# A feed-forward stage of its own for the last batch, in Q's weights and stage 1's PSUM banks, under a new order of all engines

## What is computed

```python
x = x + xattn(layernorm(x), ctx, ctx, Wq, Wk, Wv, Wo)      # softmax(q k^T / sqrt(32)) v, then Wo
n = layernorm(x).astype(bfloat16)
qg, sg = dynamic_quant(n, inv_gate)                        # round(n * inv / scale), scale = max|n * inv| / 127
qu, su = dynamic_quant(n, inv_up)
inter = silu(qg @ w_gate.T * sg * s_wgate) * (qu @ w_up.T * su * s_wup)
inter = clip(inter, -10, 10).astype(bfloat16)
qi, si = dynamic_quant(inter, inv_inter)
out = x + qi @ w_down.T * si * s_wdown
```

## Time and profile before

| | us |
|---|---|
| median of 3 runs | 737.89 (736.92 to 738.33) |
| profiled execution | 736.11 |
| its span | 734.3 |
| TensorE busy | 674.5 (92%) |
| VectorE busy | 480.8 (65%) |
| ScalarE busy | 285.5 (39%) |
| GpSimd busy | 260.3 (35%) |
| TensorE idle before its first matmul | 11.0 |

### The profile page before, as it was taken

How to read it: one execution, slowest core, us unless ns; L and a number is a source line. 1 busy time by engine, 2 the same in 40 slices (tenths; PEclk the granted TensorE clock), 3 DMA queues, 4 the chain that set the end, 5 groups by cost and what they waited for, 6 DMA issues and landing times.

```text
span 734.3 us, 14234 instructions
## 1 busy us (share of the span) xinstructions
PE 674.5 (92%) x5840; PEld 444.2 (60%) x5840; DVE 480.8 (65%) x772; ACT 285.5 (39%) x449; POOL 260.3 (35%) x207
## 2 busy tenths in 40 slices
PE   4999999999999999999999999999899989897743
PEld 3788988867767576656665656655566444443321
DVE  3664241762675585679676877787485877977763
ACT  5343212553534315253434444351524336243330
POOL 5533310030332224423523435241544436535431
PEclk9999999999999999999999999999999999999977
DMA  9778622787570242251325241334314252213000
GB/s 341 243 258 279 216 87 87 237 239 233 169 237 2 55 155 84 88 183 66 84 68 179 89 124 58 87 112 135 94 59 122 88 151 80 73 59 90 29 29 29
DMA packets 46239, 93.58 MB, mean 127 GB/s; under 512 B 6240, under 2 KB 22624, under 8 KB 46176
## 3 DMA queue, kind: packets, MB, share of 16 engines
q1 hardware_dynamic: 43872, 84.30, 37.5%
q0 software_dynamic: 2304, 8.39, 2.9%
HBM read 70.52 MB, written 22.02 MB: 126 GB/s over the span
## 4 chain that ended last, share of the span: by engine, by line
PE 76%; DVE 10%; DMA 4%; ACT 3%; issue 2%; POOL 2%; SPq 1%; POOLq 0%; DVEq 0%; ACTq 0%
PE bank L767 20%; PE bank L680 18%; PE bank L793 6%; PE bank L642 6%; PE bank L655 5%; PE bank_o L731 4%; PE bank L815 4%; PE bank_s L717 3%; PE bank_d L736 3%; PE bank_s L699 3%; DVE neg_max L2176 2%; DMA k_stack<-k_dram 2%; PE bank L665 2%; PE bank L781 2%; DVE amax L2211 1%
## 5 line engine op out<-in xcount | busy, mean ns | idle before, releaser
L680 PE MATMUL bank<-act_t_hi,wq_hi 128*128 128x256 f16 x512 | 139.7, 273 | 0.0
L680 PE MATMUL bank<-act_t_hi,wq_lo 128*128 128x256 f16 x512 | 139.5, 272 | 0.0
L680 PE MATMUL bank<-act_t_lo,wq_hi 128*128 128x256 f16 x512 | 139.4, 272 | 0.0
L2176 DVE TENSOR_REDUCE neg_max<-bank_s 128x4 f16<-128x512 f32 x128 | 83.6, 684 | 45.6 <-PE bank_s L699 45.0
L1607 ACT ACTIVATE probs<-bank_s 128x512 f32<-128x512 f32 x128 | 73.5, 601 | 54.3 <-PE bank_s L717 47.0
L2793 POOL TENSOR_TENSOR wv_hi<-wv_hi,wv_lo 128x512 f32<-128x512 f32 x28 | 37.4, 1343 | 106.2 <-DMA wv_lo<-r_dram 106.2
L1643 ACT COPY q_t<-bank 128x1024 f16<-128x1024 f16 (+1 forms) x48 | 41.7, 869 | 46.4 <-PE bank L781 28.5
L2787 POOL TENSOR_TENSOR xs<-xb,inv_up 128x1024 f32<-128x1024 bf16 x16 | 38.0, 2378 | 57.2 <-ACT code_g L1664 57.2
L680 PEld LDWEIGHTS bank<-act_t_hi,wq_hi 128*128 128x128 f16 x512 | 49.9, 98 | 11.0 <-issue 1.2
L680 PEld LDWEIGHTS bank<-act_t_lo,wq_hi 128*128 128x128 f16 x512 | 50.1, 98 | 9.9
L680 PEld LDWEIGHTS bank<-act_t_hi,wq_lo 128*128 128x128 f16 x512 | 50.0, 98 | 6.0
(11 more groups left out here) (145 smaller groups left out, 1391.7 us busy)
## 6 DMA issues: line engine op xcount, KB each, us to landing
q_stack<-q_dram SPq DMA_DIRECT2D x48, 256.0 KB, 4.5
inp<-in_x SPq DMA_DIRECT2D x16, 512.0 KB, 5.0
wv_lo<-r_dram SPq DMA_DIRECT2D x56, 128.0 KB, 2.8
x<-in_x SPq DMA_DIRECT2D x11, 512.0 KB, 4.4
out<-x POOLq DMA_DIRECT2D x11, 512.0 KB, 3.0
q_dram<-q_st_hi SPq DMA_DIRECT2D x8, 512.0 KB, 3.3
q_dram<-q_st_lo SPq DMA_DIRECT2D x8, 512.0 KB, 3.9
w_gate<-in_ctx_t SPq DMA_DIRECT2D x6, 512.0 KB, 5.1
```

What stands on the lines that cost most here:

```text
L680: ins = nc.tensor.matmul(bank[:, :, jj, :], wq_sb[a][:, 2 * item + jj, kc, :], act_t[m][:, kc, :, :], start=(kc == 0 and (a, m) == PARTS[0 ...
L2176: nc.vector.tensor_reduce(neg_max[:, c:c + REP], bank_s[g % 2][:, :].rearrange("p (j n) -> p j n", j=REP), AX_X, ALU.max, negate=True).the ...
```

## The change

Three things. First, batch 15 (`LAST`) takes its feed-forward tiles in the memory of Q's weights, with separate ones for the two sides where one tile served both, own columns in `amax`, `scale` and `rscale`, own semaphores, and the two banks of stage 1 instead of `bank3`, in the order projection, gate and up, down. The waits that only guard the shared tiles go for this batch, among them the one of `xs_` for `code`, of `ln2_apply` and `code` for `tq`, of `tanh` for `code_i` and of `gscale` for `fin_half`. Second, its last sum goes from GpSimd to VectorE, and each half of the columns is stored by SyncE as soon as it is added. Third, the lists of all five engines stand in another order, from the first call to the last. TensorE has the same 5840 matmuls.

```diff
 def place3(r, name):
+    if r == LAST:
+        return (W3 + G3 + T3).index(name)
     if name in W3:
...
 def before3(r, name):
+    if r == LAST:
+        i = place3(r, name) - 2
+        return (r, (W3 + G3 + T3)[i]) if i >= 0 else None
...
-        if 0 <= q < NB:
+        if 0 <= q < LAST:
...
-        amax = sb("amax", [P, 3], F32)
+        amax = sb("amax", [P, 6], F32)
...
-            return bank3[place3(r, name) % 2]
+            return (bank1 if r == LAST else bank3)[place3(r, name) % 2]
+        def spare(h, start, n, dt):
+            v = flat(wq_sb[h])[:, start:start + (n if dt in (F16, BF16) else 2 * n)]
+            return v if dt == F16 else v.bitcast(dt)
+        def xs_of(r, u):
+            return spare(("hi", "lo")[u], 0, D, F32) if r == LAST else xs[:, :]
+        def xb_of(r):
+            return spare("hi", 5 * D, D, BF16) if r == LAST else xb[:, :]
+        def codes_of(r, u):
+            if r == LAST:
+                return spare("hi", (6 if u == 0 else 5) * D, D, F16)
+            return codes[u][:, :]
+        def q_t_of(r, u):
+            if r == LAST:
+                return spare(("hi", "lo", "hi")[u], (7, 2, 7)[u] * D, D, F16).rearrange("p (c n) -> p c n", c=KC)
+            return q_t[:, :, :]
+        def gu_of(r, u):
+            return spare("hi", (2 + u) * D, FF, F32) if r == LAST else (g_buf, u_buf)[u][:, :]
+        def t_of(r):
+            return spare("hi", 4 * D, FF, F32) if r == LAST else t_buf[:, :]
+        def inter_of(r):
+            return spare("lo", 3 * D, FF, BF16) if r == LAST else inter[:, :]
+        def col(t, r, u):
+            return t[:, 3 + u:4 + u] if r == LAST else t[:, u:u + 1]
...
+            def store_last(n):
+                cols = slice(n * 512, (n + 1) * 512)
+                sp.wait_ge(fin_last, n + 1)
+                sp.dma_start(out[LAST][:, cols], x2_of(LAST)[:, cols]).then_inc(stored_last, 16)
...
             def bank3_free(r, name):
...
+                if before is None and r == LAST:
+                    pe.wait_ge(s1_free, N1 * PAIRS)
+                    return
...
             def qt(p, b, u):
...
+                if r == LAST:
+                    act.wait_ge(tq_last, u + 1)
                 else:
-                    if needed(2 * r + u):
+                    act.wait_ge(tq_full, 3 * r + u + 1)
...
+                if r == LAST and u == 2:
+                    act.wait_ge(gu_full, 2 * r + 1)
...
             def ln2_apply(p, b):
...
-                if needed(3 * r - 1):
+                if needed(3 * r - 1) and r < LAST:
                     dve.wait_ge(tq_full, 3 * r - 1)
-                nc.vector.tensor_scalar(xb[:, :], x2_of(r)[:, :], mv2[:, b, 0:1], rstd2[:, b:b + 1],
+                nc.vector.tensor_scalar(xb_of(r), x2_of(r)[:, :], mv2[:, b, 0:1], rstd2[:, b:b + 1],
...
+            def fin_last_(n):
+                cols = slice(n * 512, (n + 1) * 512)
+                dve.wait_ge(dn_scaled, 2 * LAST + n + 1)
+                nc.vector.tensor_tensor(x2_of(LAST)[:, cols], x2_of(LAST)[:, cols], gu_of(LAST, n),
+                                        ALU.add).then_inc(fin_last, 1)
...
             def xs_(p, b, u):
...
-                if needed(2 * r + u):
+                if needed(2 * r + u) and r < LAST:
                     pool.wait_ge(code_ready, 2 * r + u)
-                nc.gpsimd.tensor_tensor(xs[:, :], xb[:, :], inv_sb[u][:, :], ALU.mult).then_inc(xs_ready, 1)
+                nc.gpsimd.tensor_tensor(xs_of(r, u), xb_of(r), inv_sb[u][:, :], ALU.mult).then_inc(xs_ready, 1)
...
-            resid_(7, 1, 0)
-            resid_(7, 1, 1)
-            ln2_stats(7, 1)
             dn(6, 1, 0)
             dn(6, 1, 1)
+            resid_(7, 1, 0)
+            resid_(7, 1, 1)
+            ln2_stats(7, 1)
```

More of the change, by code:

```diff
@@ L2124, in _ @@
             tanh(7, 1)
+            code_i(7, 0)
+            qt(7, 0, 2)
             code_i(7, 1)
@@ L2680, in _ @@
             quant(5, 1, 0)
+            gscale(5, 0, 1)
+            swiglu(5, 0)
             max_(7, 0, 0)
+            resid_(6, 0, 0)
+            quant_i(5, 0)
             max_(7, 0, 1)
@@ L2731, in _ @@
             ln2_stats(7, 0)
+            quant(6, 1, 1)
             gscale(6, 1, 0)
```

1960 lines of the change are left out of this document (984 added, 976 removed).

## The result

The changed kernel took **727.16 us** in the median of 4 runs (726.43 to 729.37), the kernel before 737.4 us beside it: a ratio of 0.9866, 95% interval 0.9841 to 0.9892. The profiled execution took 727.02 us (span 725.2) against 736.11 (734.3), 9.1 us less where 5.0 less were forecast. The forecast time was 732.9 us, in a range from 727 to 741: the time lies at its lower end, and the change gave twice what the sum said.

A forecast was written before the change was run, and what follows sets the result against it. TensorE was taken as the bound up to nearly 650 us, then the tail's chain of waits. Terms: -10.2 tail, +0.5 dn clock, +3.2 ahead, +1.0 clock, +0.5 start = -5.0; 731.1 profiled, plus 1.8 to the median: 732.9 us, range 727 to 741.

The forecast's parts named there:

- The middle. I take 0: TensorE's idle time between 50 and 650 us: no change from the new order, bounds -5 to +6 us.
- Start: +0.5: First loads: k(0,0) starts 3.2 us later, mostly offset by earlier x; +0.5 us, bounds -2 to +3.
- Ahead of the tail: Batch 13's up rounding, held by GpSimd's norms and power, delays batch 15's projection 3.2 us; low clock separately +1.0.
- Steps 1 to 7 of the tail: Chain from batch 15's output projection to the end: 50.3 us instead of 60.5, so -10.2 us.
- Step 3: Batch 14's up rounding on VectorE waits through both back-to-back GpSimd xs of batch 15, ending at 21.9 us, not 19.2.
- The first rival: GpSimd yields the shared port after one instruction, so batch 14's and 13's roundings start 2.1 and 1.8 us sooner; 729.0 us; chance 0.15.
- Step 5's bound: In the tail: if batch 15's gate and up also run at 1.2 GHz, 3.6 us more.
- Step 6: Tail, batch 14's up scaling through batch 15's dn: 3.2 us from dn's start to the last scaling's end, at 45.7.
- Step 7: End of the tail: last add on VectorE some 0.7 us, then 3.9 us to the end, at 50.3.
- The middle that loses 5: Rival: the new order hits more queue waits over 600 us, +5, giving 737.9 us; chance 0.15.
- The clock that stays low: Rival: 1.2 GHz from batch 13's late up into batch 15's projection (mean clock under 0.75), 741.5 us; chance 0.12.
- The change that does not do what it says: Rival: VectorE's queue order loses the overlap of batches 14 and 15, half of the 10.2 gone, 738.0 us; chance 0.08.

The follow-up runs named there:

- c1: The changed kernel with the lists of before on every engine up to the first score matmuls (65 us of matmul work); 734.56 us (0.9951).
- c2: As a1, but with the new lists from 231 to 558 us of matmul work; 738.57 us (1.0006).
- a1: The changed kernel with all lists of before put back, keeping batch 15's own tiles and banks, VectorE sum and half stores; 730.96 us (0.9903).
- a4: The changed kernel with only batch 13's up-side quant on VectorE moved back ahead of batch 12's last two scalings; 725.21 us (0.9819).
- p2: 70 trials outside the kernel: one VectorE TENSOR_SCALAR beside a GpSimd row, without or with a GpSimd-issued store ahead; in one pair 1.29 us without, 7.38 with.
- d3: As a4, but with the stores of batches 12, 13 and 14 issued by SyncE instead of GpSimd; 722.86 us (0.9792).
- a2: The changed kernel with the lists of before on every engine up to ti of batch 12, new lists behind; 728.99 us (0.987).

## Why the prediction was off

Term by term, for the pair of traces that it was made for (us against the trace of before):

```
                                             forecast   measured
start                                          +0.5       -0.3
work up to ti of batch 12                       0         -2.5
to batch 15's projection                       +3.2       +4.4
clock                                          +1.0       in the rows beside it
from there to the end                          -9.7       -10.7
sum                                            -5.0       -9.1
profiled execution to the median of the runs   +1.8       +0.1
```

The forecast median, 732.9 us, was 5.7 too long. In rounded figures these are 2.5 for the middle, 1.7 for the median, 1.0 for the tail and 0.8 for the start, less 0.2 ahead of the tail. The second pair of traces reads otherwise (start -0.2, middle -0.5, to the projection +4.1, from there -9.3, sum -5.9), but its changed execution stood 4.9 us above its median. With the mean over fifteen traces for the middle (below) and over the two pairs for the rest, the four terms are -0.3, -2.9, +4.3 and -10.0, sum -8.9. The medians fell by 10.2 and 11.7 us; what the executions without a trace save beyond that is not known.

**The step that failed is "The middle. I take 0".** I argued from the fillers, which are the same in kind, and from transposes against the copies they feed (16 places against 15). Neither counts TensorE's waits. Over the six traces with the old lists and the nine with the new ones ahead of the cut (without c1 and c2), the means are 11.8, 12.3 and 12.3 us in the three stretches before, and 9.7, 7.2 and 16.6 after: -2.1, -5.1, +4.3, so -2.9 together. The bounds (-5 to +6) held it; the term was mis-sized, 0 for -2.9. In the first trace seven waits of 0.3 to 2.0 us make 6.9 of the 12.9 us between 250 and 500 (in the second seven again, 6.8), and in the change's one of 1.2 is left. Summed over that stretch, the score matmuls waited 4.8 us and 2.0 now, `ti` 1.8 and 0.1 (for a residual add). The profile puts 1.2 of the 4.8 to `max_` on VectorE and names nothing for 2.3. Between 500 and 615 `ti` went from 0 to 1.9 and the rest of the stages behind the scores grew a little each; I take it that stage 1, over some 11 us sooner now, no longer fills there; c2 against a1 fits (18.2 and 13.2 us idle), but c2 is disturbed at its cut, so this is argued and not shown. That the 5.1 between 250 and 500 come from the lists and not the tiles, a1 and c2 show; which of the calls does it was not tried.

**Start: +0.5, measured -0.3.** The first matmul now waits 10.7 us for x, then 1.1 for Wk's low part, instead of 11.0 and 2.1. Right in kind, 0.8 off.

**Ahead of the tail: right, too small.** Batch 13's rounding was indeed held by both `norm`, 2.52 us. But the late `up` ran at 1.2 GHz (3.60), which I had in the separate 1.0, and so did the projection's first 1.2 us, which cost 0.6 more. Together 5.0 against 4.2. a4 shows that this one position costs 2 us.

**Steps 1 to 7 of the tail.** Counted from the projection's start: projection done 12.9 (forecast 12.5), batch 14's rounding done 19.9 (21.9), its `up` at 22.7 (24.9), batch 15's last matmul of `up` 35.4 (35.6), its `dn` 42.2 (42.5), last scaling done 46.5 (45.7), last add done 47.2 (46.4), end 49.8 (50.3).

- *Step 3 failed.* The rounding started where it was forecast (18.6, forecast 18.4) and took 1.21 us, not 3.5. Four instructions back to back do not make the 4.85 us row; a store has to stand ahead of them. p2 shows it, and d3 against a4. (Here batch 13's store stood ahead too, but with gaps behind it.) The first rival (port given after one instruction) was right at this place, not at batch 13's rounding, and had 0.15; I had one row for its opposite, and that row held the other condition, the store in its first line.
- *Step 5's bound came true:* `gate` of batch 15 ran at 1.2 GHz (3.60 instead of 1.9), which with its slow transposes took back nearly all of the 2.0 of step 3.
- *Step 6:* from the start of `dn` to the last scaling's end 4.3 us, not 3.2: `dn` ran at 1.2 GHz (3.56 for both). The sum took 0.5 for it, of up to 1.7.
- *Step 7 was mis-sized:* from the last add to the end took 2.5 us, not 3.9; I had halved the bytes and left the issuer's share in.

So the tail's 50.3 is right partly by errors that cancel.

**The rivals.** The middle that loses 5: refuted; the middle won instead. The clock that stays low: the mean in the stretch of the projection was 0.97, far above the 0.75 from which it decides. The change that does not do what it says: refuted by the 0.2 us wait. In the other direction, I took the tail's -10.2 for the work of the order. a1 shows that about 5.6 us of it (clock aside: 3.4 up to `ti` of batch 14, 2.2 at the end) come from tiles, sum and stores with no call moved. What the new order of the tail adds to that is not shown. From `ti` of batch 12 to the end a1 takes 68.0 us and a2, with the new order, 65.9; but c2, with a1's lists there at a higher clock (`gate` of batch 15 in 1.90 us, 3.56 in a1), takes 65.5. The medians of a1 and a2 are 2 us apart, with intervals that overlap. So most of what the tail gained came with the tiles, the sum and the stores.

**The median: luck.** I added the 1.8 us by which the median of three runs stood above the profiled execution. That was chance: the profiled one had the smallest loss in its first 250 us of all traces with the old lists, and the medians of the later comparisons were 737.4 to 739.0. After the change it was 0.1.

## What to carry to other kernels

Before you put the worth of a new order at zero, list who TensorE waited for in each stretch, and take the trace more than once: here 7 us stood in seven waits of 0.3 to 2.0 us that could have been read beforehand, and one trace in six stood some 3 us beside the others. Compare the traced execution with the median, too: they were up to 4.9 us apart. When a batch is given tiles of its own, look first at the waits that the shared tiles forced (here 3.4 us) and try the old order with them. And where an engine issues a store and then works on without a gap, look at what the engine on the shared port pays: with the issue on SyncE one VectorE instruction took 1.64 us instead of 2.75. The whole kernel came out some 2 us faster (0.9792 against 0.9819, intervals that overlap), of which the port's share is not known.
